# A mixture layer and an attention layer on one core: the logarithms of the weight sums are taken once for eight chunks instead of once in each

## The reference, cut to what matters

```python
# first layer, for every position (v, h): a 128 x 128 matrix of its own
log_w = log_softmax(log(accumulators), axis=2)
prod  = einsum('vhbk,vhks->vhbs', exp(xs - x_max), exp(log_w - w_max))
out   = log(prod) + x_max + w_max          # xs: the normalised x as (v, h, b, k)
x     = x + out
# second layer, for every image: attention over its 1024 positions
A = softmax(5 * (nf @ adj_w @ nf.T - max));  h = A @ (x @ affine_w.T + affine_b)
h = leaky(layernorm(h) * ln_g + ln_b);       x = x + h
```

## Time and profile before

| | us |
|---|---|
| median of 3 runs | 1116.97 |
| lowest, highest | 1115.87, 1119.75 |
| the profiled execution, its own time | 1118.71 |
| its span | 1117.0 |
| first products of the first layer start | 57.07 |
| last products of the first layer start | 221.59 |
| last add of the first layer starts | 225.87 |

### The profile page before, as it was taken

How to read it: one execution, slowest core, us unless ns; L and a number is a source line. 1 busy time by engine, 2 the same in 40 slices (tenths; PEclk the granted TensorE clock), 3 DMA queues, 4 the chain that set the end, 5 groups by cost and what they waited for, 6 DMA issues and landing times.

```text
span 1117.0 us, 19831 instructions
## 1 busy us (share of the span) xinstructions
PE 1036.2 (93%) x7160; PEld 785.7 (70%) x7160; DVE 803.7 (72%) x1386; ACT 911.7 (82%) x1703; POOL 534.7 (48%) x266
## 2 busy tenths in 40 slices
PE   1199999958999999999999999999999999999996
PEld 0055555536778877777777777777777777887774
DVE  7723455588777777778777777777777777777767
ACT  1699999537888888888888888888888888888885
POOL 0044445503355555555555555555555555555533
PEclk9999999979999999999999999999999999999999
DMA  8989999830122222112223222222222222222212
GB/s 357 400 326 385 403 405 408 341 151 20 57 77 76 77 76 76 76 76 76 95 95 106 104 96 98 106 82 76 86 84 97 77 76 76 76 77 77 76 58 96
DMA packets 33120, 158.59 MB, mean 142 GB/s; under 512 B 4232, under 2 KB 4860, under 8 KB 22780
## 3 DMA queue, kind: packets, MB, share of 16 engines
q1 hardware_dynamic: 33020, 157.29, 37.0%
HBM read 136.45 MB, written 20.83 MB: 141 GB/s over the span
## 4 chain that ended last, share of the span: by engine, by line
PE 82%; DMA 9%; DVE 4%; ACT 2%; issue 2%; POOL 1%; SPq 1%; POOLq 0%; ACTq 0%; DVEq 0%
PE PS L1206 22%; PE PS L1207 21%; PE PS L1208 21%; DMA Wt<-acc 6%; PE PS L1224 5%; PE PS L1183 4%; PE PS L1173 3%; PE PS L1218 2%; DMA X<-x 2%; PE PS L1194 2%; DVE st L748 2%; PE PS L1212 1%; DMA NU<-factor_rows 0%; SPq L294 0%; PE PS L1239 0%
## 5 line engine op out<-in xcount | busy, mean ns | idle before, releaser
L925 DVE TENSOR_TENSOR Pl<-PS,Ph 128x512 fp32r<-128x512 f32 x512 | 348.0, 690 | 183.9 <-ACT PS L598 179.1
L598 ACT ACTIVATE PS<-PS 128x512 f32<-128x512 f32 x512 | 305.0, 609 | 9.4 <-PE PS L1208 9.4
L597 ACT ACTIVATE Ph<-PS 128x512 fp32r<-128x512 f32 x384 | 234.5, 611 | 94.4 <-PE PS L1208 91.2
L1206 PE MATMUL PS<-Ph,hh 128*128 128x512 f32 x512 | 206.4, 403 | 1.0 <-DVE Pl L925 1.0
L1206 PE MATMUL PS<-uTh,nTh 128*128 128x512 f32 x512 | 199.9, 390 | 0.9 <-DVE uTl L899 0.9
L1207 PE MATMUL PS<-Pl,hh 128*128 128x512 f32 x512 | 200.0, 391 | 0.0
L1208 PE MATMUL PS<-uTh,nTl 128*128 128x512 f32 x512 | 199.7, 390 | 0.0
L1208 PE MATMUL PS<-Ph,hl 128*128 128x512 f32 x512 | 199.6, 390 | 0.0
L1207 PE MATMUL PS<-uTl,nTh 128*128 128x512 f32 x512 | 199.6, 390 | 0.0
L420 POOL TENSOR_TENSOR hl<-X,hh 128x1024 fp32r<-128x1024 f32 (+1 forms) x33 | 77.3, 2343 | 195.3 <-ACT hh L582 169.3
L403 POOL TENSOR_TENSOR LL<-LL 128x512 f32<-128x512 f32 x64 | 82.7, 1292 | 139.2 <-ACT LL L495 139.2
(11 more groups left out here) (140 smaller groups left out, 1596.0 us busy)
## 6 DMA issues: line engine op xcount, KB each, us to landing
Wt<-acc SPq DMA_DIRECT2D x64, 1024.0 KB, 7.5
out<-X SPq DMA_DIRECT2D x38, 512.0 KB, 2.7
X<-x SPq DMA_DIRECT2D x16, 1024.0 KB, 19.7
SQ<-norm_rows SPq DMA_DIRECT2D x31, 512.0 KB, 3.5
X<-factor_rows SPq DMA_DIRECT2D x31, 512.0 KB, 4.0
NU<-factor_rows SPq DMA_DIRECT2D x31, 512.0 KB, 4.9
X<-out SPq DMA_DIRECT2D x7, 512.0 KB, 5.8
out<-X SPq DMA_DIRECT2D x2, 256.0 KB, 2.2
```

The costliest lines, as they stand in the source:

```text
L597: act.activation(Ph[:, g % RING, :], sl, ACT.Exp, scale=SHARP)
L598: act.activation(sl, sl, ACT.Exp, scale=SHARP).then_inc(weights_ready, 1)
L925: dve.tensor_tensor(Pl[:, r, :], SL[r], Ph[:, r, :].bitcast(F32), ALU.subtract)\
L1206: pe.matmul(out_, lh, rh, start=start, stop=False)
```

## The change

For groups 0 to 6 (chunks 0 to 55, GATHERED) the sums of the eight chunks go into one PSUM bank: a matrix `pick` with four columns of ones is slid along, so that chunk i of a group fills rows 4i to 4i+3 of each quarter and adds zero to the others. ScalarE then takes one logarithm of that bank for the group (logs_of_sums), TensorE transposes it (transposes_of_sums), ScalarE keeps one copy in four (keep_logs), and GpSimd subtracts it from X, four images at a time, once all chunks of the group have been added (subtract_logs). The logarithm of a chunk has 512 columns instead of 1024, and its result is transposed without a subtraction between. The last group (chunks 56 to 63) stays as before, but VectorE takes its differences. TensorE's order goes by pairs of chunks, with the transposes of two chunks behind each other, and VectorE's and ScalarE's order follows it. The batches of images have 12, 10 and 10, ScalarE also takes the statistics of image 23, and of the last ten exponentials of group 0 VectorE scales and shifts five, for which one activation of 640 columns is left. The statistics pieces of the third quarter end with chunk 59, and pieces wait for GpSimd's subtraction.

```diff
-BATCHES = ((0, 0, 12), (0, 12, 24), (0, 24, 32), (1, 0, 4), (1, 4, 32))
+BATCHES = ((0, 0, 12), (0, 12, 22), (0, 22, 32), (1, 0, 4), (1, 4, 32))
-BY_ACT = (13, 17, 25)
-ACT_UPTO = (0, 2, 3)
+BY_ACT = (13, 17, 23, 25)
+ACT_UPTO = (0, 2, 4)
+AT_ONCE = 5
...
         @block.gpsimd
-            def difference(c):
-                pool.wait_ge(logs_ready, c + 1)
-                pool.tensor_tensor(LL[:, c % 2, 0, :], LL[:, c % 2, 0, :], LL[:, c % 2, 1, :], ALU.subtract)\
-                    .then_inc(diff_ready, 1)
-            for c in range(NCH):
-                difference(c)
+            def subtract_logs(g):
+                pool.wait_ge(sum_logs_kept, g + 1)
+                pool.wait_ge(x_added, GCH * (g + 1))
+                for k in range(GCH):
+                    xg = X[:, k * IPC:(k + 1) * IPC, g * GP:(g + 1) * GP]
+                    pool.tensor_tensor(xg, xg, kept_logs(g).unsqueeze(1).broadcast_to([P, IPC, GP]), ALU.subtract)\
+                        .then_inc(subtracted, 1)
+            for g in range(NGATHER):
+                subtract_logs(g)
...
         @block.scalar
             def logs(c):
-                act.activation(LL[:, u, :, :], PS[:, 2 * u:2 * u + 2, :], ACT.Ln).then_inc(logs_ready, 1)
+                if c < GATHERED:
+                    act.activation(LL[:, u, 0, :], PS[:, 2 * u, :], ACT.Ln).then_inc(logs_ready, 1)
+                else:
+                    if c == GATHERED:
+                        act.wait_ge(sum_logs_transposed, NGATHER)
+                    if c == GATHERED + 1:
+                        act.wait_ge(subtracted, GCH * (NGATHER - 1))
+                    act.activation(LL[:, u, :, :], PS[:, 2 * u:2 * u + 2, :], ACT.Ln).then_inc(logs_ready, 1)
+            def logs_of_sums(g):
+                act.wait_ge(products_ready, GCH * (g + 1))
+                if g:
+                    act.wait_ge(sum_logs_transposed, g)
+                act.activation(sum_logs, gathered_sums(g), ACT.Ln).then_inc(sum_logs_ready, 1)
+            def keep_logs(g):
+                act.wait_ge(sum_logs_transposed, g + 1)
+                if g >= 2:
+                    act.wait_ge(subtracted, GCH * (g - 1))
+                if g == NGATHER - 1:
+                    act.wait_ge(products_ready, GCH * NGATHER)
+                act.activation(kept_logs(g).rearrange("p (i q j) -> p j q i", i=GCH, q=Q),
+                               W1.rearrange("p (j q i r) -> p j q i r", j=CJ, q=Q, i=GCH)[:, :, :, :, 0], ACT.Copy)\
+                    .then_inc(sum_logs_kept, 1)
...
+            exps(0, range(lo, hi - AT_ONCE))
+            act.wait_ge(shifted, AT_ONCE)
+            images = ET[:, 0, hi - AT_ONCE:hi, :]
+            act.activation(images, images, ACT.Exp).then_inc(exps_ready, AT_ONCE)
...
+            for c in range(0, NCH, 2):
+                if c < GATHERED:
+                    next_exps(c)
+                    next_exps(c + 1)
                 logs(c)
+                if c and c % GCH == 0:
+                    keep_logs(c // GCH - 1)
+                logs(c + 1)
+                if c < GATHERED and (c + 2) % GCH == 0:
+                    logs_of_sums(c // GCH)
...
         @block.vector
+            dve.wait_ge(stat_steps, NS * 3)
+            for b in range(B - AT_ONCE, B):
+                dve.tensor_scalar(ET[:, 0, b, :], X[:, b, 0:GP], RS[:, b:b + 1], NB[:, b:b + 1], ALU.mult, ALU.add)\
+                    .then_inc(shifted, 1)
...
+            for c in range(0, NCH, 2):
+                if c > GATHERED:
+                    difference(c - 1)
+                if c:
+                    pieces_of(c - 2)
+                    pieces_of(c - 1)
+                    add_logs(c - 2)
+                    add_logs(c - 1)
+                if c >= GATHERED:
+                    difference(c)
+            difference(NCH - 1)
+            add_logs(NCH - 2)
...
         @block.tensor
             def sums(c):
+                w = gathered_sums(g) if c < GATHERED else PS[:, 2 * u + 1, :]
+                at = 32 - COPIES - COPIES * i
+                rows = pick[:, at:at + 32] if c < GATHERED else ones[:, :]
+                start, stop = (i == 0, i == GCH - 1) if c < GATHERED else (True, True)
...
-            for c in range(NCH + 2):
-                if c < NCH:
-                    sums(c)
-                if c >= 2:
-                    transposes(c - 2)
-                if c < NCH:
-                    products(c)
+            sums(0)
+            for c in range(0, NCH, 2):
+                if c == 0:
+                    sums(1)
+                else:
+                    sums(c)
+                products(c)
+                if c:
+                    sums(c + 1)
+                    transposes(c - 2)
+                    transposes(c - 1)
+                    if c % GCH == 0:
+                        transposes_of_sums(c // GCH - 1)
+                products(c + 1)
+            transposes(NCH - 2)
+            transposes(NCH - 1)
```

More of the change, by code:

```diff
@@ L32 @@
 GCH = GP // CP
+IPC = B // GCH
+NGATHER = NPOS // GP - 1
+GATHERED = NGATHER * GCH
+COPIES = 32 // GCH
 NGR = NPOS // GP
@@ L79, in build @@
         ones = sb("ones", [P, 32])
+        pick = sb("pick", [P, 64 - COPIES])
         Whi = sb("Whi", [P, C], F32R)
@@ L382, in _ @@
             n = 0
-            for t, v in ((ident, 0.0), (same_group, 1.0), (ones, 1.0), (H, -1.0 / C), (Dm, 1.0 / C)):
+            for t, v in ((ident, 0.0), (same_group, 1.0), (ones, 1.0), (H, -1.0 / C), (Dm, 1.0 / C),
+                         (pick[:, 0:32 - COPIES], 0.0), (pick[:, 32 - COPIES:32], 1.0),
+                         (pick[:, 32:64 - COPIES], 0.0)):
                 pool.memset(t[:, :], v).then_inc(consts_made, 1)
@@ L526, in _ @@
                     statistics(2)
+                    statistics(3)
                 roots(i)
@@ L827, in _ @@
                     done.then_inc(stat_pieces, 1)
-                for at, batch in ((5, 0), (11, 1)):
+                for at, batch in ((5, 0), (10, 1)):
                     if i == at:
@@ L835, in _ @@
                         batch_variances(batch)
+                    if i == at + 2 + batch:
                         batch_scales(batch)
@@ L840, in _, with difference, closed_images @@
             batch_scales(2)
+            dve.wait_ge(stat_steps, NS * 3)
+            for b in range(B - AT_ONCE, B):
+                dve.tensor_scalar(ET[:, 0, b, :], X[:, b, 0:GP], RS[:, b:b + 1], NB[:, b:b + 1], ALU.mult, ALU.add)\
+                    .then_inc(shifted, 1)
             per = NCH // PIECES[1]
-            ipc = B // per
+            def difference(c):
+                dve.wait_ge(logs_ready, c + 1)
+                dve.tensor_tensor(LL[:, c % 2, 0, :], LL[:, c % 2, 0, :], LL[:, c % 2, 1, :], ALU.subtract)\
+                    .then_inc(diff_ready, 1)
+            def closed_images(m, i):
+                if m < PIECES[1] - 1:
+                    return range(2 * i, 2 * i + 2)
+                return range(3 * i, 3 * i + 3) if i < 8 else range(24 + 2 * (i - 8), 26 + 2 * (i - 8)) if i < 12 else ()
             def add_logs(c):
@@ L848, in add_logs, with pieces_of @@
                     .then_inc(x_added, 1)
+            def pieces_of(c):
                 m, i = divmod(c, per)
                 if m:
[L851 to L853 removed]
+                    for b in closed_images(m, i):
+                        dve.wait_ge(subtracted, GCH * (2 * m - 1) + b // IPC + 1)
                         piece(1, m - 1, b)
[L856 to L857 removed]
+            for c in range(0, NCH, 2):
[10 more added lines that the diff above has]
+            add_logs(NCH - 2)
             def last_pieces(lo, hi):
                 for b in range(lo, hi):
+                    dve.wait_ge(subtracted, GCH * (NGATHER - 1) + b // IPC + 1)
                     done = piece(1, PIECES[1] - 1, b)
@@ L1167, in sums @@
             def sums(c):
+                g, i = divmod(c, GCH)
                 u, slot = c % 2, c % WS
                 pe.wait_ge(weights_loaded[slot], 16 * (c // WS + 1))
-                if c >= 2:
+                if c < GATHERED:
+                    if i == 0 and g >= 2:
+                        pe.wait_ge(sum_logs_ready, g - 1)
+                elif c < GATHERED + 2:
+                    pe.wait_ge(sum_logs_ready, NGATHER - 1 + u)
+                else:
                     pe.wait_ge(logs_ready, c - 1)
+                w = gathered_sums(g) if c < GATHERED else PS[:, 2 * u + 1, :]
+                at = 32 - COPIES - COPIES * i
+                rows = pick[:, at:at + 32] if c < GATHERED else ones[:, :]
+                start, stop = (i == 0, i == GCH - 1) if c < GATHERED else (True, True)
                 for q in range(Q):
-                    pe.matmul(PS[32 * q:32 * q + 32, 2 * u + 1, :], ones[:, :],
-                              Wt[:, slot, q * CJ:(q + 1) * CJ, :].rearrange("k i s -> k (i s)"), start=True, stop=True)
+                    pe.matmul(w[32 * q:32 * q + 32, :], rows,
```

(1 more changed line is left out.)

51 lines of the change are left out of this document (35 added, 16 removed).

## The result

| | before | after |
|---|---|---|
| median of 5 runs each, us | 1116.97 | 1123.65 |
| lowest, highest | 1115.82, 1119.75 | 1122.07, 1125.51 |
| the profiled execution, own time (span) | 1118.71 (1117.0) | 1122.07 (1120.3) |
| first products start | 57.07 | 55.92 |
| last products start | 221.59 | 225.05 |

The ratio is 1.0062 [1.0044, 1.008]. The forecast was 1113.2 us, with a range of 1109.5 to 1117.5: the time lies outside it, and on the side that had 8% of the chance. The marks say where: the first layer starts 1.15 us earlier and starts its last products 3.46 us later.

A forecast was written before the change was run, and what follows sets the result against it. It took the first layer to be bound by the stream of weights, TensorE's period 5% shorter. Start -0.95, first chunks -0.9, stream -1.1, pairs +0.5, end -1.3 sum to -3.75: 1113.2 us against the median, range 1109.5 to 1117.5.

The forecast's parts named there:

- TensorE's work: First layer on TensorE: +0.9 us of work lies within 7.1 us of waiting for weights, 0; pairs add +0.5.
- The pairs cost once: End of first layer: transposes of chunks 60 and 61 both stand between last sums and last products, +0.5 us.
- A stall grows by at most 0.6 us: Weight slots free unevenly, leaving 6.8 us for odd chunks against 7.4 before; claimed covered by the range.
- The stream: Weight loads from 61 us on: more requests ahead might raise the rate, -1.1 us, bounds 0 and 1.9.
- Rival 2: Weight stream was held up by its requests, all of it could run at 415 GB/s: 1108.8 to 1111.6 us; 17%.
- Rival 1: Weight stream gives nothing back, loads keep their rate and TensorE's +0.9 us shows: 1115.2 to 1116.1 us; 28%.
- Start: Before the first products: new batches, image 23 on ScalarE, fewer exponentials; products start at 56.1 instead of 57.07, -0.95 us.
- First chunks: Window 54.5 to 61: second products follow at once, slots free sooner, loads find work sooner, -0.9 us.
- End: Last chunk: difference on VectorE -0.6, two of six statistics pieces done by chunk 59 -0.7; together -1.3 us.
- GpSimd: 64 differences leave the path, 56 subtractions of 1.3 us come, with time to spare: 0.
- ScalarE: Shorter logarithms, 17.3 us a group against 19.8 of TensorE, off the path: 0.
- Rival 3: GpSimd's subtractions, slow or blocking VectorE's differences in the last group, stand in front: +5, 1122 us, or +11; 10%.

The follow-up runs named there:

- late requests: Kernel before, SyncE asking for the next load once the freed chunk's logarithm is taken, not once its products are: 1134.37 us, ratio 1.0149.
- pairs with products first: Changed kernel, still by pairs of chunks, with the pair's transposes moved behind its second products: 1115.59 us, ratio 0.9977.
- products ahead of the transposes: Kernel before with one swap in TensorE's order, products(c) ahead of transposes(c-2), nothing added or left out: 1116.42 us, ratio 0.9983.
- three slots: Kernel before with three slots of weights instead of four: 1138.57 us, ratio 1.0183.
- the pairs alone: Kernel before with TensorE's order by pairs, nothing gathered, GpSimd's differences as before: 1126.32 us, ratio 1.0071.
- the second set: Later set of runs, in which the changed kernel ran again unchanged beside the kernel before: 1121.21 against 1116.73 us, ratio 1.0031.
- the start alone: Kernel before with only the new batches, image 23 on ScalarE and five shifts on VectorE: 1117.99 us, ratio 0.9995.
- start with products first: Kernel before with the change's new start and products ahead of transposes, nothing gathered: 1115.56 us, ratio 0.9975.
- the best form: Changed kernel, gathered, chunk by chunk, products ahead of transposes, last gathered logarithm put into a free part of ET: 1114.42 us, ratio 0.9962.
- the gathered form with products first: Changed kernel with gathering and subtraction kept, but chunk by chunk and products ahead of transposes: 1114.83 us, ratio 0.9978.

## Why the prediction was wrong

**The step that failed** stands under *TensorE's work*: "The pairs cost once", +0.5 us, and "A stall grows by at most 0.6 us; in the range". Its arithmetic was right and its reading wrong. It had the odd chunks' slots at 3.1 us of hold, and four periods less that, 6.8 us, "for a load that lands in 7.5". Added up instead, 7.5 + 3.1 = 10.6 us a turn is 2.65 us a chunk for the whole stream; the measured turns shown above are 10.3 and 11.9 us. A late slot isn't paid once. It makes the next request late, and a load that lands late delays the one four chunks on. From the third products to the last a chunk took (225.05 - 60.32) / 61 = 2.70 us, where before it was (221.59 - 63.18) / 61 = 2.60; that is 6.3 us, and over the 2.62 that was named as the sign of a wrong forecast. The timeline of one such pair in after shows the place, being the pattern before:

```profile
77.05 1.07 PE L1275 MATMUL PS<-Wt,pick 128*32 128x512 f32 x8
78.05 1.09 PE L1301 MATMUL PS<-ident,LL 128*128 128x128 f32 x8
...
78.97 0.60 PE L1309 MATMUL PS<-ident,LL 128*128 128x128 f32 x4
...
79.50 1.11 PE L1287 MATMUL PS<-Wt,ET 128*32 128x128 f32 x32
```

From the start of these sums to the end of the products it is 3.56 us; 0.53 of that are the gathered transposes (L1309), which stand there once in four pairs. Without them it is 3.2. That a late request costs time in each turn is shown by the run with late requests (only the request moved: slower by 1.49%) and by the pairs with products first (only the transposes moved: the loss is gone).

Each turn can be taken apart by the issues and landings in the traces, here as means over chunks 8 to 59 (us). "Hold" is from landing to the end of the products, with what the sums still waited for TensorE; "request" from there to the next issue:

| | load | hold | request | sum over slots |
|---|---|---|---|---|
| products ahead of the transposes | 8.17 | 1.99 | 0.06 | 2.56 |
| before | 7.57 | 2.81 | 0.06 | 2.61 |
| after, even chunks | 8.37 | 2.38 | 0.06 | 2.70 |
| after, odd chunks | 7.48 | 3.31 | 0.06 | 2.71 |
| late requests | 7.36 | 2.75 | 1.12 | 2.81 |
| three slots | 5.81 | 2.82 | 0.06 | 2.90 |

The prediction held the load at 7.5 us and asked whether it fits. But the load's time moves: from products first to before 0.8 us more of hold is nearly given back by a load that lands 0.6 sooner, while the late requests' 1.0 us more gets 0.2 back. In after the means are nearly those of before (hold 2.84, load 7.92), and yet it is slower. The even chunks' slots come free 0.4 us sooner, which their loads lose again (8.37 us; all loads land in the order of their issue), and the odd chunks' 0.5 us more of hold gets only 0.1 back. So a longer hold costs what the load's time no longer gives back, and adding 7.5 and 3.1 gives the direction, not the size.

**The stream** (-1.1, bounds 0 and 1.9). In 61 to 100 it gave 1.8 us, near its upper bound; behind 100 it took 6.0 back. The lower bound was missing: I excluded a loss without a reason, although a part of the change delays requests. Rival 2 had the mechanism, a stream held up by its requests, and its 415 GB/s is what the runs with products first reach; the change moved the requests the other way. Rival 1's reason, that a DMA share of 1.00 leaves no room, fell too: products first gives 415 GB/s at 1.01.

**Start** (-0.95) was right: -1.15. ScalarE's five exponentials and one of 640 columns took 2.03 and 0.72 us (forecast 1.95 and 0.71), the timeline answering to the earlier trace rows:

```profile
53.21 2.03 ACT L512 ACTIVATE ET<-X,NB,RS 128x128 f32<-128x128 f32 x5 [0.85 <-DVE NB L882]
53.21 1.37 DVE L909 TENSOR_SCALAR ET<-X,RS,NB 128x128 f32<-128x128 f32 x5
...
55.15 0.72 ACT L588 ACTIVATE ET<-ET 128x640 f32<-128x640 f32 x1
...
55.92 3.64 PE L1287 MATMUL PS<-Wt,ET 128*32 128x128 f32 x64 [0.69 <-ACT ET L588]
```

**First chunks** (-0.9) was right too: the window 54.5 to 61 moves 100 GB/s, which is 1.0 us of loads more; third products came at 60.32, forecast 59.7.

**End** (-1.3): from the last products to the first reduction 230.88 - 225.05 = 5.83 us, before 6.97: -1.14. The timeline, answering to the earlier trace rows:

```profile
225.05 1.11 PE L1287 MATMUL PS<-Wt,ET 128*32 128x128 f32 x32
...
227.28 0.69 DVE L916 TENSOR_TENSOR LL<-LL 128x512 f32<-128x512 f32 x1 [0.67 <-ACT LL L527]
227.88 1.52 DVE L927 TENSOR_TENSOR X<-PS,X 128x512 f32<-128x512 f32 x2
...
229.44 1.41 DVE L813 BATCH_NORM_STATS2 st<-X 128x6 f32<-128x256 f32 x4
230.88 0.20 DVE L838 TENSOR_REDUCE gsum<-st 128x4 f32<-128x32 f32 x1
```

**GpSimd** (0) held: 48 of the subtractions took 1.29 us each, the eight beside VectorE's differences up to 1.73, and cutting them changed nothing. **ScalarE** (0) held for the change, busy 82% in 100 to 180; that it would be on the path without the shorter logarithm was seen only in the pairs alone. Rival 3 did not come.

The sum in the profiles: start -1.15, stream +4.61 (3.46 + 1.15), end -1.14, together +2.3, which is how much later the second layer's first queries are taken (246.41 against 244.12). Another 1.0 us comes behind, by the clock: +3.3, the difference of the spans. The medians differ by 6.7 us and, in the second set, by 4.5; the profiled execution of after was its fastest. So the sum explains the profiled pair, and about half of what the first medians show.

**What stays open.** The same stream landed differently in different runs of after (its last window had 375 GB/s in one profile, 410 in another), so the loss has a spread of some 3 us between two sets of runs that no run explains. The loads come in less regularly in the two runs with the latest requests: the time from landing to landing has a standard deviation of 0.50 us with late requests and 0.59 with three slots, 0.36 in before and 0.37 in after, 0.27 in the third run (products first). Why isn't known.

## What to carry to other kernels

Where loads pass through few slots, write down for each slot its whole turn: request to landing, plus landing to release. Compare the longest with slots times the stream's period, also where the mean is unchanged. The time to landing in this sum is no constant, so the comparison tells where to look, and a run has to tell how much. The last reader of a slot goes as early in its engine's order as it can, ahead of work that only finishes an older chunk. A large share of loads in the chain of waits is read with the releases between them: if those are long, the order is to be changed, and if they are short, as in the pairs with products first, the stream is near the highest rate that any run reached (413 GB/s there, 415 at most in the same window).

## What the runs showed of the hardware

**A full queue isn't shown by the DMA share.** Before had a share of 1.00 at 403 GB/s in 100 to 180 and products first 1.01 at 415; after 0.99 at 392. So 6% of the rate lie within 0.02 of the share.

**The load's time adapts to the slots.** It was 7.5 us with four slots and 5.7 with three, so a load's time to landing is no constant to be set against a hold.

**The clock in the second layer's opening.** Three windows of before, then of after (the third number from the end is the granted clock):

```profile
258.00:260.00 2.00, 0.09 (x1) 0.00 (x0) 1.88 (x4) 1.57 (x4) 1.56 (x1) 1.00 0.00 0
262.00:266.00 4.00, 4.00 (x18) 3.00 (x17) 3.90 (x9) 2.87 (x7) 0.00 (x0) 1.00 0.02 4
266.00:270.00 4.00, 4.00 (x19) 3.31 (x18) 2.68 (x5) 3.90 (x7) 1.14 (x1) 1.00 0.23 65
```

```profile
260.00:262.00 2.00, 0.38 (x2) 0.00 (x0) 1.59 (x4) 1.86 (x4) 1.85 (x1) 1.00 0.00 0
262.00:266.00 4.00, 2.97 (x15) 2.15 (x16) 3.97 (x8) 0.07 (x1) 0.00 (x0) 0.80 0.00 0
266.00:270.00 4.00, 4.00 (x15) 3.13 (x15) 3.28 (x9) 3.36 (x7) 0.00 (x0) 0.78 0.02 4
```

After TensorE had idled for most of 260 to 262, the clock was at its lower level of 1.2 GHz for some 3.4 us (0.2 x 4 / 0.5 + 0.22 x 4 / 0.5). In before it idled as much from 258 to 260, and the clock stayed at 1.00, so this idle stretch alone doesn't decide it. The way from the first to the third query step took 22.8 us with such a stretch and 21.8 without. It came in ten of the profiles, among them that of the start alone, whose gain of 1.0 us it ate. In two of the ten (start with products first, and the best form) it was twice as long and the way took 23.6 and 23.7 us. It did not come in those of before, the pairs alone, the three slots and the gathered form with products first, all at 21.8. It isn't the change's own, and what decides whether it comes is open.
